# A fused transformer kernel: ties at the 32nd score found by counting, and one stage's weights loaded a stage earlier

## The chip, the cores and the metric

The kernel runs on one core of a Trainium2 chip, as one program of five instruction streams: TensorE (PE in the rows, PEld its weight loads), VectorE (DVE), ScalarE (ACT), GpSimd (POOL) and SyncE (SP, which only issues transfers). The metric is the device time of one execution in microseconds; lower is better. The kernel before took 2199.34 us in the median of three runs (2195.12 to 2203.02).

## The reference, cut to what matters

Six blocks follow each other, each on a layer norm of the running sum `x` (4 batches of 256 tokens, 256 wide):

```python
x = x + _L0_xattn_ref(_layernorm(x), ctx_768, ...)   # cross attention
x = x + _L0_attn_ref(_layernorm(x), ...)             # linear attention, a scan over tokens
x = x + _L0_ffn_ref(_layernorm(x), ...)              # 8 experts with low-rank parts
x = x + _L1_xattn_ref(_layernorm(x), ctx_768, ...)   # top-32 cross attention, S4D
x = x + _L1_attn_ref(_layernorm(x), ...)
x = x + _L1_ffn_ref(_layernorm(x), ...)
```

The change touches the fourth block's attention. There each query of each of 4 heads scores 4096 context rows, keeps the 32 best and takes their softmax:

```python
scores = jnp.einsum('bthd,bghd->bhtg', Q, K) / np.sqrt(DH)
topv, topi = jax.lax.top_k(scores, K_TOP)            # K_TOP = 32
probs = jax.nn.softmax(topv, axis=-1)
attn = jnp.zeros_like(scores).at[bi, hi, ti, topi].set(probs)
attn_mean = attn.mean(axis=1)                        # over the heads
c_t = jnp.einsum('btg,bgd->btd', attn_mean, V)
```

The expert block picks one expert for each token by the largest logit. The S4D part of the fourth block needs a convolution kernel that depends on weights alone; it is computed early, beside the experts.

## The kernel before, in words

`build` makes a list of stages: `stage_x0` (first cross attention), `stage_hla` (linear attention), `stage_moe` (experts, the S4D kernel, and the first keys of the next stage), `stage_x1a` (selection), then `stage_x1b` and `stage_a1`. Each stage has one function per engine. Between stages, `stage_end` lets every engine wait until all of them are done. Nothing is reordered: each engine runs its instructions as the code writes them, and waits on semaphores (`e.wait_ge`) are written by hand. SP issues its transfers in its own order, with waits of the same kind.

**Experts (`stage_moe`).** A list `plan`, made by `woven`, interleaves four strands: the experts of two batches, again two batches, the S4D kernel, and the keys ("keys" jobs, 8 chunks of 512 columns). SP begins with three loads of packed weights: `x1a` (weights of the keys), `moe` and `s4d`. Then it issues the context for the key chunks (`key_projection`, tiles `CT0` and `CT1` in turn, each waiting until the product that read it two pieces before is done). In the plan, DVE does the norms of two batches first, then the S4D set-up (`z_dt` on ACT, `z_pi` on DVE), then the first angle, then the gate's arithmetic (L1338). PE does two key chunks, transposes, two key chunks, then the gate products.

**Selection (`stage_x1a`).** There are 16 passes `p`: 4 batches x 2 halves of the tokens x 2 pairs of heads. A pass has two heads `h` with 128 queries in the partitions. PE computes 128x4096 scores per head and ACT copies them to SBUF (`SC`, two buffers). For each head DVE takes the 8 largest of each of 32 groups of 128 scores (`candidates`, L1674, results in `CA`, 128x256), and then `top` finds the 32 largest among the 256 candidates: MAX8 gives 8 values, MATCH_REPLACE overwrites these with `SENT`, and so on. `top` in the kernel before goes four rounds past the first MAX8, so that it has 40 values, and sets a flag where the 33rd value is not below the 32nd (a tie) or where some group of 128 holds 8 values that all reach the 32nd (a group may then hold more). PE adds up the flags of both heads over the partitions, DVE reads the sum into a register (`check`), and if it isn't zero a slow branch selects again with full-width passes. ACT computes the exponentials into `PM` (`weigh`), and DVE's `select` (L1716) masks and sums them: `(SC >= 32nd value) * PM`, 4096 wide, for both heads. POOL then takes, for each head, the reciprocal of the sum (L1787), scales (L1792 or L1795, into `ACC` or in place) and adds to `ACC` (L1797).

DVE's order for step `n`: candidates of pass `n-1`, first head; within them, after group 16 or 32, `check` and `select` of pass `n-2`; `top`; the second head's candidates; `top`. The select of an odd pass comes after 16 of the 32 groups, that of an even pass after all 32. Before three of the steps DVE converts a mask (L1667, 32x128), before three others it normalises a batch for the next queries (L1660).

## Time and profile before

| | us |
|---|---|
| median of 3 runs | 2199.34 |
| profiled execution | 2203.82 |
| its span, first to last instruction | 2202.0 |

| stretch, us from the span's start | what | length |
|---|---|---|
| to 889 | first cross attention | 889 |
| 889 to 1092.4 | linear attention (DMA share 0.01 between 1000 and 1060) | 203 |
| 1092.4 to 1250 | experts, S4D kernel, first keys | 158 |
| 1250 to about 1834 | selection | 584 |
| to 2202 | the rest | 368 |

Over the whole span PE is busy for 82%, DVE 56%, ACT 47%, POOL 35%. Such shares say little by themselves: each stretch has its own limit, and what a change is worth is read in its own stretch. A row of a timeline gives the start and the length of an instruction (or of several alike, with their count), and in brackets how long the engine was idle before it and what ended that. Idle time of an engine that isn't the bottleneck costs nothing.

### The profile page before, as it was taken

The page shows a single profiled execution, that of the slowest core. Times are in us where ns is not written, and L with a number is a line of the kernel's source. Part 1 is how long each engine was busy: PE and PEld are TensorE (multiplying, and loading weights), DVE is VectorE, ACT ScalarE, POOL GpSimd, SP SyncE. Part 2 cuts the span into 40 slices and gives each one's busy share as a digit, 9 for nine tenths or more (in the row PEclk, how much of TensorE's full clock was granted, in tenths as well). Part 3 has the DMA queues.
Part 4 walks back from the last instruction along what each step waited for, and adds up shares of the span by engine and source line. Part 5 has one row for each costly group of instructions (what it writes and reads, how often), then busy time and mean ns, then how long its engine had stood idle before and what let it go on. Part 6 is the DMA issues. An engine that isn't in the chain of part 4 may idle for free. (4 is left out here: it accounts for less than half of the span.)

```text
span 2202.0 us, 34851 instructions
## 1 busy us (share of the span) xinstructions
PE 1807.5 (82%) x13676; PEld 1104.1 (50%) x13676; DVE 1233.7 (56%) x3075; ACT 1025.5 (47%) x1381; POOL 759.8 (35%) x669
## 2 busy tenths in 40 slices
PE   5969999999999898888687877877766849888874
PEld 2434554454445444556466723544444437676653
DVE  5142424333332300364578379899999995557675
ACT  1457657756765687112131145555546521214442
POOL 6343324433542230000030027777878850110000
PEclk8989999999999999999967855878787669999897
DMA  6647555655756170000120001223132252000000
GB/s 143 118 105 127 117 109 109 117 119 113 122 109 128 56 125 38 1 2 1 58 70 1 14 1 44 79 59 87 51 86 66 58 184 86 1 1 1 1 6 15
DMA packets 78046, 150.01 MB, mean 68 GB/s; under 512 B 15464, under 2 KB 63144, under 8 KB 71464
## 3 DMA queue, kind: packets, MB, share of 16 engines
q1 hardware_dynamic: 64304, 101.80, 16.5%
q0 software_dynamic: 12768, 42.59, 12.7%
q8 instruction: 118, 1.93, 0.4%
q10 hardware_dynamic: 792, 3.17, 0.4%
q14 instruction: 64, 0.52, 0.1%
HBM read 93.59 MB, written 2.62 MB: 44 GB/s over the span
## 5 line engine op out<-in xcount | busy, mean ns | idle before, releaser
L571 ACT ACTIVATE P<-R 128x1024 f32<-128x1024 f32 x512 | 506.8, 1026 | 222.3 <-PE R L112 186.3
L112 PE MATMUL R<-QS,KST 100*128 100x256 bf16 x2048 | 297.0, 277 | 60.2 <-ACT P L571 53.5
L112 PEld LDWEIGHTS R<-QS,KST 100*128 100x128 bf16 x2048 | 170.0, 98 | 224.8 <-ACT P L571 120.9
L1797 POOL TENSOR_TENSOR ACC<-ACC,PM 128x4096 f32<-128x4096 f32 x22 | 195.2, 8872 | 1.8
L200 POOL TENSOR_TENSOR LNrs<-LNve,pk_const 128x2 f32<-128x2 f32 x36 | 25.3, 703 | 462.7 <-DVE LNve L196 462.5
L112 PE MATMUL R<-OV,QT 32*128 32x512 f32 x512 | 183.0, 802 | 0.0
L789 POOL DMA_DIRECT2D KST<-OV x300 | 144.5, 490 | 71.7 <-PE R L112 55.2
L112 PE MATMUL R<-P,VP 128*32 128x256 f32 x2304 | 156.1, 388 | 5.3 <-issue 5.0
L601 DVE CAST OV<-RT 128x512 bf16<-128x512 f32 x64 | 27.7, 432 | 217.2 <-ACT RT L116 130.0
L733 POOL CAST OV<-RT 128x512 bf16<-128x512 f32 x64 | 42.6, 665 | 266.5 <-DVE RT L604 266.5
L1787 POOL TENSOR_TENSOR SM<-SM,NG 128x1 f32<-128x1 f32 x30 | 79.3, 2644 | 147.5 <-DVE PM L1716 147.5
L112 PE MATMUL B<-P,VP 128*32 128x256 f32 x1792 | 121.2, 388 | 0.0
L1674 DVE MAX8 CA<-S 128x8 f32<-128x128 f32 x512 | 101.8, 275 | 12.0 <-ACT S L116 11.6
L1674 DVE MAX8 CA<-SC 128x8 f32<-128x128 f32 x512 | 100.9, 277 | 4.8 <-ACT SC L116 4.1
L116 ACT ACTIVATE S<-R 128x1024 f32<-128x1024 f32 x64 | 64.1, 1023 | 60.1 <-DVE PM L1716 34.3
L112 PEld LDWEIGHTS R<-P,VP 128*32 128x32 f32 x2304 | 60.7, 109 | 61.9 <-issue 36.2
L112 PE MATMUL R<-OV,ONB 1*128 1x512 bf16 x256 | 62.9, 488 | 33.9 <-ACT SC L116 20.8
L112 PEld LDWEIGHTS R<-OV,QT 32*128 32x128 f32 x512 | 65.1, 251 | 38.7 <-issue 30.9
L112 PE MATMUL R<-CN,AT 128*128 128x192 f32 x288 | 67.0, 385 | 19.1 <-DMA CN<-in_ctxn 13.6
L116 ACT ACTIVATE SC<-R 128x1024 f32<-128x1024 f32 x64 | 64.1, 1020 | 39.6 <-PE R L112 24.3
L1795 POOL TENSOR_SCALAR PM<-PM,SM 128x4096 f32<-128x4096 f32 x22 | 80.9, 3679 | 2.2
L1716 DVE SCALAR_TENSOR_TENSOR PM<-SC,T,PM 128x4096 f32<-128x4096 f32 x16 | 71.1, 4484 | 9.8 <-ACT S L116 4.2
(370 smaller groups left out, 3559.0 us busy)
## 6 DMA issues: line engine op xcount, KB each, us to landing
KST<-OV POOLq DMA_DIRECT2D x276, 128.0 KB, 10.8
CT<-in_ctxP SPq DMA_DIRECT2D x40, 768.0 KB, 4.4
CN<-in_ctxn SPq DMA_DIRECT2D x60, 384.0 KB, 3.5
CT<-in_ctxT SPq DMA_DIRECT2D x64, 192.0 KB, 2.5
KST<-OV SPq DMA_DIRECT2D x84, 128.0 KB, 10.4
KST<-in_ctxP ACTq DMA_DIRECT2D x4, 768.0 KB, 9.4
QS<-x_q POOLq DMA_DIRECT2D x24, 128.0 KB, 5.4
pk_a<-in_pk_a SPq DMA_DIRECT2D x1, 3014.0 KB, 10.4
```

Source lines behind the costliest of these rows:

```text
L112: return e.matmul(o, l, r, start=st, stop=sp, skip_group_check=True)
L116: return e.activation(o, i, ACT.Copy)
L200: return e.tensor_tensor(LNrs[:, i, :], LNve[:, i, :], cst["nhalf"], ALU.pow)
L571: e.activation(P[(32 * p + k0) % 3][:, :], ring.at(("s", p, k0))[:, :], ACT.Exp).then_inc(*EX.up((p, k0)))
L601: e.tensor_copy(KS[0][:, cs], rt[:, :]).then_inc(*KD.up())
L733: e.tensor_copy(KS[1][:, cs], rt[:, :]).then_inc(*KG.up())
L789: e.dma_start(KST[buf][16 * s:16 * s + 16, hh, cols], KS[SLOT_K[s]][r0:r0 + 16, cols]).then_inc(*S[buf].up((b, g) if hh == hs[-1] and s == ...
L1674: e.max(CA[:, g * 8:g * 8 + 8], SC[p % 2][:, h, g * 128:g * 128 + 128]).then_inc(*V.up())
L1716: e.scalar_tensor_tensor(pm[:, :], SC[p % 2][:, h, :], T8[p % 2][:, h, 31:32], pm[:, :], ALU.is_ge, ALU.mult, accum_out=SM[p % 3][:, h, SU ...
L1787: e.tensor_tensor(rc, sm[:, h, SUM:SUM + 1], NG1[:, :], ALU.pow).then_inc(*G.up())
L1795: e.tensor_scalar(pm, pm, rc, 0.25, ALU.mult, ALU.mult).then_inc(*G.up())
L1797: e.tensor_tensor(acc[:, :], acc[:, :], pm, ALU.add).then_inc(*G.up(("sum", p, h)))
```

## The change

In `top`, the fourth round (MATCH_REPLACE and MAX8) goes. In its place a TENSOR_SCALAR compares all 256 remaining candidates with the 32nd value and adds up the result along the row. 24 of the 32 largest have been overwritten by then, so the count is 8 where there is no tie. The last instruction becomes a SCALAR_TENSOR_TENSOR, which compares the largest eighth value of a group with the 32nd, as before, and adds the count. Summed over 128 rows and two heads, the value without ties or full groups is 2 x 128 x 8, and `check` compares with that.

In `stage_moe`, the three loads and the context of the first key chunk move to a new function, `moe_loads`, whose `sync` SP runs in `stage_hla`. Its order is `s4d`, `x1a`, `moe`, context. The tiles are allocated ahead of the linear attention's and kept through both stages. `key_projection` takes the PSUM slots as an argument of its functions; its instructions are the same.

```diff
-        def stage_hla(c):
+        def stage_hla(c, loads):
 ...
             def sync(e):
-                pass
+                loads(e)
 ...
+        def moe_loads(c, x1a):
+            t = {nm: pack(c, nm) for nm in ("moe", "s4d")}
+            keys = key_projection(c, x1a[1])
+            LW, W4 = dsig("w_moe"), dsig("w_s4d")
+
+            def sync(e):
+                load(e, "s4d", t["s4d"][0], W4)
+                load(e, "x1a", x1a[0], LA)
+                load(e, "moe", t["moe"][0], LW)
+                keys["sync"](e, 0, 0)
+
+            return dict(t, keys=keys, LW=LW, W4=W4, sync=sync)
 ...
             def sync(e):
-                load(e, "x1a", x1a[0], LA)
-                load(e, "moe", t_moe, LW)
-                load(e, "s4d", t_s4, W4)
                 for kind, *at in plan:
-                    if kind == "keys":
+                    if kind == "keys" and at[1] > 0:
                         keys["sync"](e, *at)
 ...
-                    for r8 in range(4):
+                    for r8 in range(3):
                         if r8 > 0:
                             e.wait_ge(*V.now())
                         e.match_replace(CA[:, :], t8[:, 8 * r8:8 * r8 + 8], CA[:, :], SENT).then_inc(*V.up())
                         e.wait_ge(*V.now())
                         e.max(t8[:, 8 * r8 + 8:8 * r8 + 16], CA[:, :]).then_inc(*V.up())
+
                     e.wait_ge(*V.now())
-                    e.tensor_scalar(fl, fl, t8[:, 32:33], t8[:, 31:32], ALU.max, ALU.is_ge).then_inc(*V.up(("fl", p, h)))
+                    e.tensor_scalar(CA[:, :], CA[:, :], t8[:, 31:32], 0.0, ALU.is_ge, ALU.add, accum_out=t8[:, 32:33]).then_inc(*V.up())
+                    e.wait_ge(*V.now())
+                    e.scalar_tensor_tensor(fl, fl, t8[:, 31:32], t8[:, 32:33], ALU.is_ge, ALU.add).then_inc(*V.up(("fl", p, h)))
 ...
-                    with e.If_ne(reg["v"], 0):
+                    with e.If_ne(reg["v"], 2 * 128 * 8):
```

On DVE, the end of `top` for the first pass and head stands like this before (`CA` are the candidates, `T_143` the values found, `SM_145` holds the flag):

```order
L1686 MATCH_REPLACE CA<-T_143,CA 128x256 [waits x1_select]
L1688 MAX T_143<-CA 128x8 [waits x1_select]
L1686 MATCH_REPLACE CA<-T_143,CA 128x256 [waits x1_select]
L1688 MAX T_143<-CA 128x8 [waits x1_select]
L1690 TENSOR_SCALAR SM_145<-SM_145,T_143 128x1 [waits x1_select]
L1674 MAX CA<-SC_127 128x8 [waits x1_copy,x1_select]
```

and like this in the changed kernel:

```order
L1696 MATCH_REPLACE CA<-T_143,CA 128x256 [waits x1_select]
L1698 MAX T_143<-CA 128x8 [waits x1_select]
L1701 TENSOR_SCALAR CA,T_143<-CA,T_143 128x256 [waits x1_select]
L1703 SCALAR_TENSOR_TENSOR SM_145<-SM_145,T_143 128x1 [waits x1_select]
L1684 MAX CA<-SC_127 128x8 [waits x1_copy,x1_select]
```

One MATCH_REPLACE and one MAX are replaced by the count, and the last instruction before the next candidates has two tensors as inputs, `SM_145` and a column of `T_143`, beside the scalar from `T_143`. Before, it had one tensor and two scalars.

On SP, at the end of the first cross attention, before (`OV<-in_pk_hla` is the linear attention's weights, issued in the first stage):

```order
L222 DMA OV<-in_pk_hla 128x4864 [waits d_k_slots1,d_k_slots_pool1,d_k_slots_pool0,d_k_slots0]
L222 DMA pk_x1a<-in_pk_x1a 128x512 [waits stage_end_tensor,stage_end_vector,stage_end_gpsimd,stage_end_scalar]
L222 DMA pk_moe<-in_pk_moe 128x5512
L222 DMA pk_s4d<-in_pk_s4d 128x1291
L1067 DMA CT_91<-in_ctxT 96x2x256
L1067 DMA CT_92<-in_ctxT 96x2x256
L1067 DMA CT_91<-in_ctxT 96x2x256 [waits x1_key_product]
```

and in the changed kernel:

```order
L222 DMA OV<-in_pk_hla 128x4864 [waits d_k_slots1,d_k_slots_pool1,d_k_slots_pool0,d_k_slots0]
L222 DMA pk_s4d<-in_pk_s4d 128x1291 [waits stage_end_scalar,stage_end_gpsimd,stage_end_vector,stage_end_tensor]
L222 DMA pk_x1a<-in_pk_x1a 128x512
L222 DMA pk_moe<-in_pk_moe 128x5512
L1082 DMA CT_52<-in_ctxT 96x2x256
L1082 DMA CT_53<-in_ctxT 96x2x256
L1082 DMA CT_52<-in_ctxT 96x2x256 [waits stage_end_gpsimd,stage_end_scalar,x1_key_product,stage_end_vector,stage_end_tensor]
```

The waits for the ends of the stages show where the boundary lies: the five transfers stand behind the first boundary only, and the sixth behind the second as well.

## Rows read from the trace of the kernel before

**Rows 1.** Windows view, 1250:1850: busy us (count) by engine, clock, DMA share.

```profile
1250.00:1850.00 600.00, 444.52 (x1879) 268.47 (x1880) 526.04 (x1695) 300.58 (x269) 389.03 (x89) 0.73 0.24 74
```

**Rows 2.** Timeline, DVE, one odd and one even pass: start us, length us.

```profile
1604.59 4.49 DVE L1716 SCALAR_TENSOR_TENSOR PM<-SC,T,PM 128x4096 f32<-128x4096 f32 x1 [0.59 <-DVE FI L1697]
...
1620.23 0.09 DVE L1686 MATCH_VALUE_LOAD CA<-T,CA 128x8 f32 x1
...
1621.21 0.27 DVE L1690 TENSOR_SCALAR SM<-SM,T 128x1 f32<-128x1 f32 x1
...
1621.52 6.29 DVE L1674 MAX8 CA<-S 128x8 f32<-128x128 f32 x32
...
1632.42 0.27 DVE L1690 TENSOR_SCALAR SM<-SM,T 128x1 f32<-128x1 f32 x1
...
1639.65 4.52 DVE L1716 SCALAR_TENSOR_TENSOR PM<-S,T,PM 128x4096 f32<-128x4096 f32 x1 [0.59 <-DVE FI L1697]
...
1653.19 0.27 DVE L1690 TENSOR_SCALAR SM<-SM,T 128x1 f32<-128x1 f32 x1
...
1664.40 0.27 DVE L1690 TENSOR_SCALAR SM<-SM,T 128x1 f32<-128x1 f32 x1
...
1669.38 4.49 DVE L1716 SCALAR_TENSOR_TENSOR PM<-SC,T,PM 128x4096 f32<-128x4096 f32 x1 [1.44 <-ACT S L116]
```

**Rows 3.** Timeline, POOL, the same stretch.

```profile
1617.75 8.91 POOL L1797 TENSOR_TENSOR ACC<-ACC,PM 128x4096 f32<-128x4096 f32 x1
...
1627.27 3.69 POOL L1795 TENSOR_SCALAR PM<-PM,SM 128x4096 f32<-128x4096 f32 x1
...
1631.04 8.84 POOL L1797 TENSOR_TENSOR ACC<-ACC,PM 128x4096 f32<-128x4096 f32 x1
...
1652.79 0.55 POOL L1787 TENSOR_TENSOR SM<-SM,NG 128x1 f32<-128x1 f32 x1
...
1657.20 8.89 POOL L1797 TENSOR_TENSOR ACC<-ACC,PM 128x4096 f32<-128x4096 f32 x1
```

**Rows 4.** Timeline, all engines, start of the expert stage.

```profile
1097.21 0.73 DVE L204 TENSOR_SCALAR XN<-X,LNmv,LNrs 128x256 f32<-128x256 f32 x2 [0.81 <-POOL LNrs L200]
...
1104.23 0.42 ACT L1212 ACTIVATE z_dt<-pk_s4d 128x256 f32<-128x256 f32 x1 [16.57 <-DMA pk_s4d<-in_pk_s4d]
...
1104.75 0.42 DVE L1292 TENSOR_TENSOR z_pi<-z_dt,pk_s4d 128x256 f32<-128x256 f32 x1 [6.81 <-ACT z_dt L1212]
...
1109.61 0.43 DVE L1246 TENSOR_TENSOR z_den<-z_t,z_t 128x256 f32<-128x256 f32 x1
...
1120.34 0.57 ACT L116 ACTIVATE OV<-B 128x512 f32<-128x512 f32 x1
...
1122.26 3.47 PE L112 MATMUL B<-pk_moe,XT 128*128 128x40 f32 x16
...
1124.13 0.24 DVE L1338 TENSOR_TENSOR LG<-B,pk_moe 128x80 f32<-128x80 f32 x1 [4.88 <-PE B L112]
```

**Rows 5.** Groups by line and form, DVE: busy us, mean ns.

```profile
L1716 DVE DVE_READ_ACCUMULATOR PM<-S,T,PM 128x1 f32 x16 | 1.3, 81 | 0.0
...
L1300 DVE TENSOR_SCALAR z_nden<-z_den 128x256 f32<-128x256 f32 x1 | 0.3, 293 | 0.0
```

**Rows 6.** One source line, L647: ns min/median/max.

```profile
L647 DVE TENSOR_TENSOR BW<-KMX,QMX x8: 149/159/987, 42.3 to 770.3; 128x1 f32<-128x1 f32 x8
```

**Rows 7.** Timeline, POOL and DVE, 42:44.

```profile
42.16 1.15 POOL L735 TENSOR_TENSOR OV<-RT,OV 128x512 bf16<-128x512 f32 x1
42.34 0.99 DVE L647 TENSOR_TENSOR BW<-KMX,QMX 128x1 f32<-128x1 f32 x1
```

**Rows 8.** Timeline, POOL and DVE, near 1599.

```profile
1591.88 8.88 POOL L1797 TENSOR_TENSOR ACC<-ACC,PM 128x4096 f32<-128x4096 f32 x1
...
1599.27 1.57 DVE L1667 TENSOR_SCALAR MR<-MU 32x128 bf16<-32x128 uint8 x1
```

**Rows 9.** DMA issues: KB, median us to landing.

```profile
pk_moe<-in_pk_moe SPq DMA_DIRECT2D x1, 2756.0 KB, 9.2
```

More of the change, by code:

```diff
@@ L1051, in sync, with key_projection @@
             def sync(e):
-                pass
+                loads(e)
             return dict(tensor=tensor, vector=vector, scalar=scalar, gpsimd=gpsimd, sync=sync, slots=(ring, bank))
-        def key_projection(c, w, bank):
+        def moe_loads(c, x1a):
[8 more added lines that the diff above has]
+            return dict(t, keys=keys, LW=LW, W4=W4, sync=sync)
+        def key_projection(c, w):
             K1 = OV[:, 0:NK]
@@ L1067, in sync, with tensor @@
                     e.dma_start(CT[n % 2][:, :, :], src).then_inc(*CT1[n % 2].up(n))
-            def tensor(e, b, ch):
+            def tensor(e, bank, b, ch):
                 ps, free = bank.take(("k", b, ch), (KC1, (b, ch)))
@@ L1077, in tensor, with scalar @@
                     mm(e, o, w["Wk"][0:96, 1, :], CT[n % 2][:, 1, :], False, True).then_inc(*KM1.up(n))
-            def scalar(e, b, ch):
+            def scalar(e, bank, b, ch):
                 e.wait_ge(*KM1.at(16 * b + 2 * ch + 1))
@@ L1083, in key_projection, with stage_moe @@
             return dict(tensor=tensor, scalar=scalar, sync=sync)
-        def stage_moe(c, x1a):
-            t_moe, w = pack(c, "moe")
+        def stage_moe(c, early):
+            w, ws, keys, LW, W4 = early["moe"][1], early["s4d"][1], early["keys"], early["LW"], early["W4"]
             XN = [sbt(c, f"XN{i}", [128, 2, 256]) for i in range(2)]
@@ L1094, in stage_moe @@
             ring, bank = Slots(R), Slots(B2)
-            keys = key_projection(c, x1a[1], bank)
-            t_s4, ws = pack(c, "s4d")
             zs = ["dt", "pr", "pi", "den", "nden", "nr", "t0", "t1", "cr", "ci", "dr", "di", "b0"]
@@ L1105, in stage_moe @@
             z = {k: v[:, :] for k, v in Z.items()}
-            M, V, S, NP, GZ, LW = sig("moe_product"), sig("moe_vector"), sig("moe_inter"), sig("moe_root"), sig("moe_zero"), dsig("w_moe")
-            W4, V4, S4, G4, M4 = dsig("w_s4d"), sig("s4d_vector"), sig("s4d_function"), sig("s4d_outer"), sig("s4d_kernel")
+            M, V, S, NP, GZ = sig("moe_product"), sig("moe_vector"), sig("moe_inter"), sig("moe_root"), sig("moe_zero")
+            V4, S4, G4, M4 = sig("s4d_vector"), sig("s4d_function"), sig("s4d_outer"), sig("s4d_kernel")
             s4_steps = 15
@@ L1142, in tensor @@
                             e.wait_ge(*LA.at("x1a"))
-                        keys["tensor"](e, *at)
+                        keys["tensor"](e, bank, *at)
                     elif kind == "s4d" and at[0] == "kernel":
@@ L1208, in scalar @@
                     if kind == "keys":
-                        keys["scalar"](e, *at)
+                        keys["scalar"](e, bank, *at)
                     elif kind == "s4d" and at[0] == "setup":
@@ L1419, in stage_x1a @@
             ring, bank = Slots(R[0:2]), Slots([B2[0], B2[1], R[2][:, 0:512], R[2][:, 512:1024]])
-            keys = key_projection(c, w, bank)
+            keys = key_projection(c, w)
             K1, MRT = OV[:, 0:NK], OV[:, NK:NK + NK // 2].bitcast(BF16)
@@ L1576, in tensor @@
                         if n % 4 == 0 and rekeyed(n, ch):
-                            keys["tensor"](e, *rekeyed(n, ch))
+                            keys["tensor"](e, bank, *rekeyed(n, ch))
                         if n < NP:
@@ L1580, in tensor @@
                         if n % 4 == 3 and rekeyed(n, ch):
-                            keys["tensor"](e, *rekeyed(n, ch))
+                            keys["tensor"](e, bank, *rekeyed(n, ch))
                         if m is not None and n % 2 == 0 and ch in (1, 3, 5, 7):
@@ L1642, in scalar @@
                         if n % 4 == 0 and rekeyed(n, ch):
-                            keys["scalar"](e, *rekeyed(n, ch))
+                            keys["scalar"](e, bank, *rekeyed(n, ch))
                         if n < NP:
@@ L1646, in scalar @@
                         if n % 4 == 3 and rekeyed(n, ch):
-                            keys["scalar"](e, *rekeyed(n, ch))
+                            keys["scalar"](e, bank, *rekeyed(n, ch))
                         if m is not None and n % 2 == 0 and ch in (3, 5):
@@ L2592, in build @@
             stages.append(stage_x0(c))
-        with ExitStack() as c:
-            stages.append(stage_hla(c))
         KL = sbt(ctx, "KL", [128, 2, 256])
         x1a = pack(ctx, "x1a")
-        with ExitStack() as c:
-            stages.append(stage_moe(c, x1a))
+        with ExitStack() as both:
+            early = moe_loads(both, x1a)
+            with ExitStack() as c:
+                stages.append(stage_hla(c, early["sync"]))
+            with ExitStack() as c:
+                stages.append(stage_moe(c, early))
         CS = sbt(ctx, "CS", [128, 2 * NB, 192])
```

## The prediction

> **What bounds the kernel now.** I read the time of each stretch first, then the timeline of VectorE (DVE) in the two stretches that the change touches, then GpSimd (POOL) beside it. The selection stage lies between 1250 and 1850 us. DVE is busy 526 of its 600 us, PE 445, POOL 389, ACT 301 [rows 1], so DVE sets the pace, and the reader is to see that POOL is busy two thirds of the time beside it. DVE's order repeats every two passes [rows 2]. In an odd pass the masked sums ("select", L1716) come in the middle of the first candidate sweep, in an even pass at its end. From the select at 1604.59 (odd) to the one at 1639.65 (even) it is 35.06 us, from there to 1669.38 it is 29.73. DVE hardly idles; before 1669.38 it waits 1.44 for ACT.
>
> Each select releases POOL, which then runs without a gap [rows 3]: a small power instruction, a scaling (3.7 us), a 4096-wide addition (8.9), and for the second head all three again. After the odd select it ends at 1639.88, where the even select has just begun. So POOL's chain (35.3 from select to end) is as long as DVE's half period (35.06).
>
> The expert stage starts at 1092.4 with nothing loaded. ACT's first instruction waits for the S4D pack until 1104.23, DVE starts its S4D arithmetic at 1104.75 although its norms were done at 1097.94 [rows 4].
>
> **The change, part by part.**
>
> *Fourth round removed.* A round is MATCH_VALUE_LOAD, MATCH_REPLACE and MAX8: from 1620.23 to 1621.21, 0.98 us. The flag instruction L1690 goes too, 0.31 by the start of the next one [rows 2]. Removed: 1.29 us in each of 32 calls of `top`, 41.3 us of DVE.
>
> *Count added.* A TENSOR_SCALAR of 128x256 with an accumulated output. No row shows this form. Below it lies the plain one at 0.29 [rows 5], above it an instruction with two inputs of this width, 0.43 [rows 4]. I take 0.42 (the upper row, since the one accumulated form that the trace has, the select, runs at one element a cycle: 4.49 us for 4096), plus 0.08 for reading the accumulator [rows 5], plus 0.1 to the next start: 0.6.
>
> *Combining flag added.* A SCALAR_TENSOR_TENSOR of 128x1 on the flag and the count, both in SBUF. By itself 0.16, the median of L647's 128x1 TENSOR_TENSOR [rows 6], 0.25 with the gap. If nothing interfered, `top` would be 1.29 - 0.6 - 0.25 = 0.44 us shorter, 14 us in all.
>
> It is interfered with. L647 runs eight times: 0.16 in the median, 0.99 at most [rows 6]. The longest starts at 42.34 while POOL adds from 42.16 to 43.31, and ends at 43.33, with POOL's instruction [rows 7]. So a DVE instruction with two SBUF tensor inputs, however small, waits for the whole POOL instruction in flight. The selection shows the same for another form: the 32x128 mask conversion L1667 takes 1.57 beside an addition on POOL from 1591.88 to 1600.76 and ends with it [rows 8]. The old flag instruction had one tensor and pointer scalars and took 0.27 in the middle of POOL's additions (at 1621.21, 1632.42 and 1664.40 [rows 2, 3]): it was not held. The new one, with two tensors, stands exactly there. Behind it in DVE's queue are all candidates, the next select, and by that POOL, ACT's copies into the score buffer and PE's flag product.
>
> The odd half: three rounds end at 1620.23, the count takes 0.6, and the flag wants to start at 1620.85. POOL adds from 1617.75 to 1626.66 [rows 3]: a wait of 5.8. The next candidates start at 1626.9, not 1621.52 (+5.4). The second `top` arrives 5.4 later, less 0.4 saved, so its flag wants to start at 1637.4; POOL's second addition ends at 1639.88, moved 0.2 by the flag let in before it: a wait of 2.7. Candidates start at 1640.3, not 1632.73. The half is longer by 7.6. There are seven (passes 1, 3, ... 13; pass 15 has no successor on POOL): 7 x 7.6 = 53.
>
> The even half: the first flag wants to start at 1652.8, at a small power instruction (1652.79, 0.55 [rows 3]): at most 0.5 lost, as much as was saved. The second wants 1664.0 and POOL adds until 1666.09: a wait of 2.2, candidates 1.7 later. But before the next select DVE waited 1.44 for ACT, which hides that, and in five of the eight even halves a conversion or a norm already waits for this same addition [rows 8], so that they grow by only 0.3. I take 4 for all. Selection: +57, with 49 to 62 as its bounds: 7 x 6.7 to 7 x 8 (the count from 0.29 to 1.0 shifts little, since it lies under the wait; POOL's next instruction may slip in first, 0.6), and 2 to 6 for the even halves. PE and ACT, busy 445 and 301 of 600, get more slack, not less.
>
> The Trainium skill, "SBUF — State Buffer", Who interferes with whom, says that a TENSOR_SCALAR which also writes out its accumulator stays out of the two-port mode, and so would not be held by POOL; no run here shows it. By the rule the count costs what I put down; were it to behave like L1667, the rival below holds.
>
> *Loads moved.* In the expert stage SP issues three packs and the first keys' context. They now go at the start of the linear attention, which lasts 203 us, with a DMA share of 0.01 in the middle of it (the table above). SP has nothing else queued there, and waits at the stage's end in any case. I cost the four pieces at nothing: the largest has 2756 KB and lands in 9.2 us [rows 9]. If that cover were gone, at worst all of these 9.2 us would fall on the linear attention's start and take the gain below with them. At the expert stage's start, DVE goes on to S4D at 1097.95 in place of 1104.75: 6.8 gained. The 4.88 us that it waited before L1338 are for the gate product; this waits for ACT's copy of keys (1120.34), which sits behind ACT's sines, which wait for DVE. All these move by 6.8, but PE is then early: the gate product can start at the copy's end (1120.9 - 6.8 = 1114.1) rather than at 1122.26 [rows 4], so it gains 8.2. I take 8; bounds 0 (the cover gone) and 11.7 (6.8 and all of the 4.88). After that PE, ACT and DVE hand on to each other and all move alike.
>
> **Sum.** Against the profiled execution, 2203.8 (span 2202.0 and 1.8 around it): + 57 - 8 = 2252.8. It is 4.5 above the median of the three runs, 2199.3, so the median comes out at 2199.3 + 49 = 2248.
>
> **Rivals.**
> 1. *Small flags aren't held* (L647's 0.99 would then be chance). For: a single instance. Against: it ends with POOL's instruction to 0.02 us, and the 0.84 too much are too large for noise. Then DVE has 14 us less. But POOL's chain of 35.3 leaves the odd halves where they are, since the select has two SBUF tensors itself and would wait for it; and the masks and norms wait for the end of the addition anyway. That leaves some 1 us for each of the three last even halves: -2.5 - 8 = -10.5, 2189. This is the faster side, and it decides by one thing: the wait of the 128x1 form. If nothing were held, not even the select, it would be -14 - 8, 2177.
> 2. *The count is held too*, by using both ports like L1667. It then waits first, POOL's next instruction slips in, and the flag waits again. What changes is that the count's own 0.5 us no longer lies under the wait, in some 28 of the 32 calls: 14 more, 2262.
> 3. *The fall-back runs*, because the count isn't 2048 in sum over both heads. The branch has 16 full-width instructions for each pass; at the select's 4.4 us each, 70 us a pass, and above 3300 for all 16. The diff's arithmetic gives 8 per row and head without ties, so I give it 2 in 100.
> 4. *The waits cancel*: the added 7.6 lie where PE and ACT were already late, or the early loads disturb less than they save. Price: around 2205. For it speaks only that DVE idles a few us per pass; against it that it hardly idles in the rows.
>
> **Chances.** Forecast 0.74, rival 1 0.13, rival 2 0.08, rival 3 0.02, rival 4 0.03. The forecast's own range is 2236 to 2258. With 2 in 10 left out the range takes in rival 2 and the lower end of the main case: 2226 to 2266. A change of 0.3% (6.6 us) is what the measurement can tell. Slower: forecast, rivals 2 and 3, 0.84; same: 0.03; faster: 0.13.
>
> **What would show it.** Right: 32 flag instructions of 128x1 whose durations are mostly 2 to 6 us and end with POOL's additions; odd halves of 42 to 43 us; L1667 no longer near 1.6; 96 MATCH_REPLACE; counts at 0.4 to 0.5. Expert stage: S4D's first DVE instruction 5.5 us after the stage's start (was 12.4), the stage 8 us shorter, the linear attention unchanged. Wrong: flag instructions of 0.2 us beside a busy POOL, or DVE idle for ACT or PE where I have it held.

## The result and the profile after

| | before | after |
|---|---|---|
| median of the paired runs, us | 2198.47 (4 runs) | 2235.97 (2234.02 to 2238.47, 4 runs) |
| ratio | | 1.017, 95% interval 1.0147 to 1.0192 |
| profiled execution / its span | 2203.82 / 2202.0 | 2234.31 / 2232.5 |
| linear attention | 203.1 | 201.6 |
| expert stage | 158.6 | 149.8 |
| selection | 582.9 | 630.8 |
| the rest | 368.0 | 365.4 |

The change costs 37.5 us, 1.7%. I had forecast +49. Both terms show: the selection is 47.9 longer (forecast 57), the expert stage 8.9 shorter (forecast 8; from DVE's last addition to `X` in one stage to that in the next it is 157.92 before and 149.07 after). The two profiled executions differ by 30.5, less than the medians: the one after was quicker by 8.6 ahead of and behind the two stages, 4.5 of it in the first cross attention, whose code is the same.

The selection by engine, as in [rows 1], now from 1250 to 1850 of the changed kernel:

```profile
1250.00:1850.00 600.00, 417.26 (x1713) 247.67 (x1710) 561.62 (x1592) 291.29 (x254) 384.10 (x82) 0.70 0.22 66
```

DVE is busy 562 of 600 in place of 526, with fewer instructions (1592 for 1695), and PE, ACT and POOL do less in the same time. "Busy" includes the time in which an instruction has started and is held; a higher share is not more work.

DVE's instructions of the selection in the changed kernel, grouped (busy us, mean ns of one):

```profile
L1703 DVE SCALAR_TENSOR_TENSOR SM<-SM,T 128x1 f32<-128x1 f32 x32 | 84.1, 2630 | 1.1
...
L1696 DVE MATCH_REPLACE8 CA<-T,CA 128x256 f32<-128x256 f32 x96 | 39.2, 409 | 0.0
L1701 DVE TENSOR_SCALAR_CACHE_REDUCE CA<-CA,T 128x256 f32<-128x256 f32 x32 | 15.3, 479 | 1.1
```

One element per partition, 32 times, is 84.1 us, more than twice what all 96 MATCH_REPLACE of 256 elements cost. The count has a mean of 479 ns.

One odd half of the changed kernel on DVE, which answers to [rows 2]:

```profile
1320.36 4.48 DVE L1729 SCALAR_TENSOR_TENSOR PM<-SC,T,PM 128x4096 f32<-128x4096 f32 x1 [0.91 <-DVE FI L1710]
...
1335.99 0.48 DVE L1701 TENSOR_SCALAR_CACHE_REDUCE CA<-CA,T 128x256 f32<-128x256 f32 x1
1336.52 5.87 DVE L1703 SCALAR_TENSOR_TENSOR SM<-SM,T 128x1 f32<-128x1 f32 x1
1342.42 6.29 DVE L1684 MAX8 CA<-S 128x8 f32<-128x128 f32 x32
...
1352.86 2.76 DVE L1703 SCALAR_TENSOR_TENSOR SM<-SM,T 128x1 f32<-128x1 f32 x1
1355.65 6.28 DVE L1684 MAX8 CA<-SC 128x8 f32<-128x128 f32 x32
...
1362.88 4.48 DVE L1729 SCALAR_TENSOR_TENSOR PM<-S,T,PM 128x4096 f32<-128x4096 f32 x1 [0.90 <-DVE FI L1710]
```

and POOL beside it, which answers to [rows 3]:

```profile
1324.94 4.72 POOL L1800 TENSOR_TENSOR SM<-SM,NG 128x1 f32<-128x1 f32 x1 [8.79 <-DVE PM L1729]
...
1333.52 8.85 POOL L1810 TENSOR_TENSOR ACC<-ACC,PM 128x4096 f32<-128x4096 f32 x1
...
1346.74 8.86 POOL L1810 TENSOR_TENSOR ACC<-ACC,PM 128x4096 f32<-128x4096 f32 x1
```

Add start and length. The first flag ends at 1342.39, POOL's first addition at 1342.37; the second flag ends at 1355.62, the second addition at 1355.60. From the flag's start to the addition's end it is 5.85 and 2.74 (forecast 5.8 and 2.7). So it is with all: of the 32 flags 22 take 2.6 to 5.9 us, and each of these ends 0.01 to 0.03 us after an addition of POOL; the other ten take 0.22 and meet no addition. POOL is idle 8.79 before it starts: it waits for the DVE that it holds up later. The count at 1335.99 runs in the middle of the same addition and isn't held.

The holding goes both ways. POOL's first small instruction, 128x1 with two inputs in SBUF, takes 4.72 at 1324.94, beside DVE's second select, where its neighbours of the same shape take 0.55. The "35.3 from select to end" of POOL's chain includes these 4 us too.

The start of the expert stage, after, which answers to [rows 4] (the last instruction of the linear attention on DVE is the first row):

```profile
1085.52 0.69 DVE L1043 TENSOR_TENSOR X<-B,X 128x512 f32<-128x512 f32 x1 [5.89 <-PE B L112]
...
1091.84 0.42 DVE L1305 TENSOR_TENSOR z_pi<-z_dt,pk_s4d 128x256 f32<-128x256 f32 x1
...
1108.26 0.24 DVE L1351 TENSOR_TENSOR LG<-B,pk_moe 128x80 f32<-128x80 f32 x1 [3.75 <-PE B L112]
```

`z_pi` follows the norms with no wait. The gate's arithmetic (L1351) starts 22.7 after that first row, where it was 32.6 before (1091.54 to 1124.13 in [rows 4]).

### The profile page after: what moved, and what is told of

Read it like the earlier page. It is cut to its first block, busy times and chain, and to the rows that moved or that the text cites. A ratio compares the mean times of both kernels' runs of the same rounds, so it can differ in the third digit from the quotient of the medians.

```text
span 2232.5 us, 34819 instructions
## 1 busy us (share of the span) xinstructions
PE 1811.9 (81%) x13676; PEld 1108.1 (50%) x13676; DVE 1286.1 (58%) x3043; ACT 1025.9 (46%) x1381; POOL 760.7 (34%) x669
## 4 chain that ended last, share of the span: by engine, by line
PE 47%; DVE 31%; ACT 10%; issue 5%; POOL 3%; DMA 3%; DVEq 0%; ACTq 0%; POOLq 0%
PE R L112 30%; PE B L112 15%; DVE CA L1684 7%; ACT P L571 7%; DVE PM L1729 6%; DVE SM L1703 3%; POOL KST L789 2%; DMA KST<-OV 2%; DVE CA L1696 2%; DVE T L1698 2%; PE B L178 1%; ACT PS L2367 1%; DVE RT L604 1%; ACT RT L116 1%; DMA CN<-in_ctxn 1%
## 5 line engine op out<-in xcount | busy, mean ns | idle before, releaser
L112 PE MATMUL R<-OV,QT 32*128 32x512 f32 x512 | 188.2, 823 | 0.0
L1703 DVE SCALAR_TENSOR_TENSOR SM<-SM,T 128x1 f32<-128x1 f32 x32 | 84.1, 2630 | 1.1
L116 ACT ACTIVATE SC<-R 128x1024 f32<-128x1024 f32 x64 | 64.0, 1020 | 38.7 <-PE R L112 22.7
```

The costliest lines, as they stand in the source:

```text
L112: return e.matmul(o, l, r, start=st, stop=sp, skip_group_check=True)
L116: return e.activation(o, i, ACT.Copy)
L1703: e.scalar_tensor_tensor(fl, fl, t8[:, 31:32], t8[:, 32:33], ALU.is_ge, ALU.add).then_inc(*V.up(("fl", p, h)))
```

## The experiments

Twelve kernels, with the kernel before run beside each. The two columns on the right are parts of the profiled execution: the selection, here from DVE's last addition to `X` in the expert stage to the first scaling of `OV` after the selection (1.7 more than in the table above, by its start), and the last stretch, from there to the end of the span.

| kernel | time, us | ratio to before | selection | last stretch |
|---|---|---|---|---|
| before | | 1 | 584.6 | 368.0 |
| after | 2235.97 | 1.017 (1.0147 to 1.0192) | 632.5 | 365.4 |
| e1 scalar flag | 2183.96 | 0.9942 (0.9928 to 0.9956) | 581.2 | 365.1 |
| e2 loads only | 2188.57 | 0.9954 (0.9940 to 0.9969) | 585.1 | 367.9 |
| e3 old rounds, two-tensor flag, late loads | 2247.78 | 1.0224 (1.0210 to 1.0238) | 632.9 | 367.6 |
| e4 POOL's addition in quarters | 2186.05 | 0.9951 (0.9937 to 0.9965) | 585.3 | 364.7 |
| e5 scalar flag and quarters | 2182.37 | 0.9932 (0.9906 to 0.9957) | 581.4 | 365.3 |
| e6 scalar flag, late loads | 2190.03 | 0.9967 (0.9956 to 0.9979) | 581.5 | 365.1 |
| e7 POOL's addition in halves | 2207.09 | 1.0037 (1.0022 to 1.0051) | 605.5 | 365.1 |
| e8 old rounds, early loads, quarters | 2195.66 | 0.9998 (0.9986 to 1.0011) | 590.1 | 368.2 |
| e9 scalar flag, half of the addition | 2178.42 | 0.9906 (0.9878 to 0.9935) | 577.9 | 365.4 |
| e10 old rounds, early loads, half of the addition | 2184.05 | 0.9934 (0.9912 to 0.9956) | 579.8 | 368.3 |
| e11 scalar flag, 32 fillers | 2182.44 | 0.9938 (0.9921 to 0.9954) | 582.5 | 364.3 |
| e12 scalar flag, 8 fillers | 2180.66 (one run) | | 581.3 | 365.2 |

The kernels ran in four groups (e1 to e4, e5 to e8, e9 and e10, e11 and e12), so ratios are compared across groups, not times.

### Is it the form of the flag?

**e1**, the changed kernel with one line changed:

```diff
-e.scalar_tensor_tensor(fl, fl, t8[:, 31:32], t8[:, 32:33], ALU.is_ge, ALU.add)
+e.tensor_scalar(fl, fl, t8[:, 31:32], t8[:, 32:33], ALU.is_ge, ALU.add)
```

> The changed kernel with one instruction in another form: the flag is combined by a TENSOR_SCALAR with the 32nd value and the count as pointer scalars, instead of a SCALAR_TENSOR_TENSOR with two SBUF tensors. Same values, same waits. Theory (a DVE instruction with two SBUF tensors waits for the whole POOL instruction in flight): the 32 flags take 0.27 us each, the selection falls from 630.8 us to 580 (the 583 of before, less some 3 for the round saved, since POOL's chain sets the odd halves), the kernel comes to 2198 - 9 - 3 = 2186 (2182 to 2191). Rival (the count itself, 0.56 us with its accumulator, and the extra semaphore hop are what costs): the time stays near 2236.

Measured 2183.96. The groups of e1 in the selection:

```profile
L1701 DVE TENSOR_SCALAR_CACHE_REDUCE CA<-CA,T 128x256 f32<-128x256 f32 x32 | 15.3, 479 | 1.1
L1703 DVE TENSOR_SCALAR SM<-SM,T 128x1 f32<-128x1 f32 x32 | 8.7, 273 | 1.2
```

The same two values reach the instruction, the count now through a pointer scalar in place of a tensor operand. The flags fall from 84.1 to 8.7 us and the kernel by 52. The count stays at 479: it was never held.

**e3**, the kernel before with only the form of its flag changed:

```diff
-e.tensor_scalar(fl, fl, t8[:, 32:33], t8[:, 31:32], ALU.max, ALU.is_ge)
+e.scalar_tensor_tensor(fl, fl, t8[:, 32:33], t8[:, 31:32], ALU.max, ALU.is_ge)
```

> The kernel before with one instruction in another form: its flag (four rounds, no count, late loads) is a SCALAR_TENSOR_TENSOR with two SBUF tensors instead of a TENSOR_SCALAR with two pointer scalars. Same values. Theory: as the saved 0.4 us per call lie under the waits, this form alone costs 50 (45 to 57): 2248, flags of 5.5, 2.5, 0.3 and 2.5 us in turn. Rival (the count is needed for the loss): 2198 and flags of 0.3 us.

Measured 2247.78, against 2198.09 before in the same group: +49.7. The group of e3:

```profile
L1690 DVE SCALAR_TENSOR_TENSOR SM<-SM,T 128x1 f32<-128x1 f32 x32 | 70.2, 2193 | 1.1
```

The form alone makes the loss, on a kernel with no other change. Together e1 and e3 settle it from both sides. They change the operation and the number of tensor operands at once; that it is the operands is argued, from the TENSOR_TENSOR of 128x1 in [rows 7], which was held as well.

**e2**, the changed kernel with the old selection, so the early loads alone:

> The changed kernel with the selection of the kernel before (four rounds, old flag); only the loads are early. Theory: expert stage 149.8 us as in the changed kernel (158.7 before), all else as before: 2198 - 9 = 2189 (2186 to 2193). Rival (the linear attention pays for the transfers, or later stages give the gain back): 2198.

Measured 2188.57, 9.5 under the kernel before in its group (by the interval of the ratio 7 to 13).

**e6**, the other half: the selection of e1, with the loads issued at the start of the expert stage, in the old order:

> The count with the scalar flag, and the loads issued at the start of the expert stage in the order of the kernel before. Theory: the two parts of the change add up, so that the time is that of the scalar flag with early loads (2184) plus the 8.9 that the expert stage lost: 2192.5 (2190 to 2196), expert stage at 158 to 159, S4D's first DVE instruction 12.4 after its start, selection at 579.6. Rival, that part of the gain seen in the expert stage is given back or taken elsewhere (transfers on top of the linear attention, other addresses in SBUF): the time is below 2188 or above 2197, with the difference outside of the expert stage.

Measured 2190.03, at the edge of the range. By the ratios it is 5.5 above e1 (by their intervals 1.5 to 9.5) where I expected 8.9. The expert stage took 156.0 in e6's profile (from DVE's last addition to `X` in the linear attention to its last one in the expert stage), 147.7 in e1's and 157.9 in before's, so that e6 and e1 differ by 8.3 there. Its first S4D instruction starts 12.8 after the stretch's start (13.2 before). But the gate's arithmetic in e6 came 30.2 after the start and not 32.6. PE, the gate products in before and in e6:

```profile
1122.26 3.47 PE L112 MATMUL B<-pk_moe,XT 128*128 128x40 f32 x16
```

```profile
1114.37 1.98 PE L112 MATMUL B<-pk_moe,XT 128*128 128x40 f32 x16 [0.36 <-ACT OV L116]
```

The same products take 3.47 at a granted clock of 0.50 and 1.98 at 1.00. In e6 the clock was at 1.00 in the two groups of key products ahead of them too; in before it was 0.79 in the first of these and 0.56 in the second. So the early loads are worth 5.5 to 9.5, by which neighbour they are taken against, and e6's expert stage is 1.9 shorter than that of before, which comes with the higher clock.

### Does a held instruction wait for the POOL instruction in flight?

**e7 and e4** cut POOL's addition of 4096 columns into two of 2048 and four of 1024, and keep the two-tensor flag:

```diff
-e.tensor_tensor(acc[:, :], acc[:, :], pm, ALU.add).then_inc(*G.up(("sum", p, h)))
+for q4 in range(4):
+    qs = slice(q4 * NK // 4, (q4 + 1) * NK // 4)
+    e.tensor_tensor(acc[:, qs], acc[:, qs], pm[:, qs], ALU.add).then_inc(*G.up(("sum", p, h) if q4 == 3 else None))
```

> The changed kernel with its two-tensor flag, POOL's 4096-wide addition as two of 2048 (4.5 us each). Theory: a held flag ends with the POOL instruction in flight, so no flag takes over 4.6 us, and they end with the first or the second half of an addition; total of the flags between the 26.6 us of quarters and the 84.1 of whole additions, 40 to 60; time between 2186 and 2236, 2200 (2192 to 2212). Rival, that a held instruction waits until POOL has nothing more to do, or for a fixed time: durations as in the changed kernel, or the same in halves and quarters (up to 1.7).

> The changed kernel with POOL's 4096-wide addition as four of 1024, one after another with no wait between them; the two-tensor flag stays. Theory (the hold lasts as long as the one POOL instruction in flight): no flag takes over 2.5 us, and the kernel is at 2200 (2193 to 2210), POOL's chain being some 0.5 us longer per addition. Rival (the hold lasts until POOL's queue is empty, or it is something else): flags up to 5.9 us, 2236 or more.

Measured 2207.09 in halves, 2186.05 in quarters. The flags' groups of e7 and of e4:

```profile
L1703 DVE SCALAR_TENSOR_TENSOR SM<-SM,T 128x1 f32<-128x1 f32 x32 | 56.0, 1751 | 1.1
```

```profile
L1703 DVE SCALAR_TENSOR_TENSOR SM<-SM,T 128x1 f32<-128x1 f32 x32 | 26.6, 830 | 1.1
```

The flags take 84.1, 56.0, 26.6 us for whole, half and quarter instructions, and 2236, 2207, 2186 for the kernel. In e7 a flag and POOL's two halves (9.02 us for both) look like this:

```profile
1611.36 1.55 DVE L1703 SCALAR_TENSOR_TENSOR SM<-SM,T 128x1 f32<-128x1 f32 x1
```

```profile
1608.37 9.02 POOL L1812 TENSOR_TENSOR ACC<-ACC,PM 128x2048 f32<-128x2048 f32 x2
```

The flag ends at 1612.91, and the first half, half of 9.02 from 1608.37, at 1612.88. DVE gets in between two POOL instructions; a held instruction waits for one instruction, not for the end of POOL's work. The longest flags fall from 5.9 to 2.9 and 1.7. POOL pays little for the cut: 9.3 for four quarters in place of 8.87.

e4 beat my 2200 because the even halves fell too, those without keys from 30.3 to 28.4: their second flag's wait of 2.7 is also cut, to 0.8, and I had counted the odd halves alone.

### Why is the saved round worth so little once the flag is cured?

The count takes 0.42 us per `top` off DVE, 13.4 in all (DVE's busy time in e9 against e10, below). Against e2 (old rounds) e1 is only 4.6 faster, 2.6 by the ratios. Three pairs that differ by the count alone:

| POOL's addition | with the count | old rounds | difference of ratios x 2198 | difference of the selections |
|---|---|---|---|---|
| whole | e1, 0.9942 | e2, 0.9954 | 2.6 (4.4 either way) | 3.8 |
| in quarters | e5, 0.9932 | e8, 0.9998 | 14.5 (6 either way) | 8.8 |
| half left out | e9, 0.9906 | e10, 0.9934 | 6.2 (8 either way) | 1.9 |

Only the middle difference of ratios is clear of the noise. The selections of the profiles tell more, and each pair differs by another 2.9 in the last stretch (the last experiments below).

> The changed kernel with both cures: the flag as a TENSOR_SCALAR with two pointer scalars, and POOL's 4096-wide addition as four of 1024. With the scalar flag alone the odd halves were 34.13 from the start of one select to the next, but the even select was then held 0.94 us by POOL's addition, so that from end to end it is 35.07: POOL's chain still bounded them. With the quarters alone they were 36.16, of which 2.0 are waits of the flags. Theory: with both, nothing on DVE waits more than a quarter of an addition, so odd halves are 34.1 to 34.3, even halves 28 (28.4 less 0.6 of flags' waits), and the kernel is 16 to 20 us below the 2186 of the quarters alone, less 3 to 8 us of waits for ACT and PE that come back: 2172 (2166 to 2180). Rival, that POOL's chain bounds the halves whether cut up or not (its additions in quarters take 9.3 in place of 8.9, 36.1 for the chain): odd halves stay at 36.1 and the time at 2184 to 2186, in spite of flags of 0.27.

> The old selection (four rounds, old flag) with the early loads, and POOL's addition in quarters. It completes a square with the loads only (2189), the scalar flag (2184) and both cures together. Theory: the count saves 0.4 us per call where POOL no longer holds DVE, 14 us in all, of which 2184 against 2189 shows only 5, because the select is held by POOL's addition there. So here the time is 8 to 14 us above that of the scalar flag with quarters: 2183 (2178 to 2188). Rival, that the small gain of the count lies in waits for ACT and PE, which the quarters don't change: the difference between the two kernels with quarters is again 5 us or less.

e5 took 2182.37, not 2172, and e8 2195.66, not 2183. Both theories of e5 are off in part. The first: the odd halves are 34.14 from start to start, as expected, but the select that follows is held. A select of e1 and one of e5, each the first of an even pass:

```profile
1621.32 5.45 DVE L1729 SCALAR_TENSOR_TENSOR PM<-S,T,PM 128x4096 f32<-128x4096 f32 x1 [0.59 <-DVE FI L1710]
```

```profile
1619.06 6.28 DVE L1729 SCALAR_TENSOR_TENSOR PM<-S,T,PM 128x4096 f32<-128x4096 f32 x1 [0.59 <-DVE FI L1710]
```

An undisturbed one takes 4.48. In e1 34.13 and 0.97 of holding make 35.10, the 35.06 of the kernel before: DVE is earlier, and meets POOL's last addition. In e5 34.14 and 1.80 make 35.94, since POOL in quarters needs 0.9 longer, and DVE comes at the last quarter. So POOL's chain from select to select bounds the odd half, in one piece or in four. That was the step in the prediction's first rival. In e8 the old rounds come at 35.06, into the same last quarter, and lose up to 0.8 there. In the kernel before they come just when POOL is through (4.52 in [rows 2]). By this luck e2's selection is 5 us shorter than e8's (the holds of e8's selects sum to 5.1), and so the pair in quarters shows more than the others; the whole difference between e2 and e8 is 9.7 by the ratios, 4.2 either way, and what lies beyond the 5 isn't explained.

The selects are not all that is held. The mask conversions and the norms of the queries in the selection (TENSOR_SCALAR, 32x128 and 128x256) have one tensor as input, and still end with POOL's additions. The three conversions beside an addition take 1.5 to 1.6 each in e2 and 2.4 to 2.5 in e1, where 0.21 is undisturbed; the two norms beside one take 1.6 to 1.7 in e2 and 2.6 in e1, where 0.41 is undisturbed. From e2 to e1 the holds grow by 5.8 for the selects, 2.8 for the conversions and 1.9 for the norms: 10.4 of the 13.4 that the count takes off. DVE's busy time in the selection falls by 3.2 alone (515.4 to 512.2). So with whole additions most of the saving goes into waits for POOL.

**e9 and e10** take the load away. POOL adds only the first 2048 columns to `ACC`:

```diff
-e.tensor_tensor(acc[:, :], acc[:, :], pm, ALU.add).then_inc(*G.up(("sum", p, h)))
+e.tensor_tensor(acc[:, 0:NK // 2], acc[:, 0:NK // 2], pm[:, 0:NK // 2], ALU.add).then_inc(*G.up(("sum", p, h)))
```

> The changed kernel with the scalar flag, and POOL adds only the first 2048 of 4096 columns to ACC (the sum over the heads is left out for the others): its chain from a select to the end of the second addition falls from 35.3 to about 26.5 us. Theory: POOL's chain bounds the selection with the scalar flag from two sides, the even select (held up to 1.8) and PE's transposes of ACC (PE waits 6.7 to 8.7 for POOL's last addition every second pass, and its score products behind them feed ACT and so DVE). With the short chain both go: odd halves 34.1 with selects of 4.5, even halves about 28, 62 for two passes in place of 65.3, 7.5 times, so 2160 (2154 to 2168), and PE no longer waits for POOL. Rival, that PE's or ACT's own work bounds the two passes at 65: no more than 4 us faster than the 2184 of the whole addition.

> The old rounds and the old flag with the early loads, and the same half addition on POOL (the sum over the heads left out for the other columns). Theory: where POOL's chain doesn't bound, the count is worth what it takes off DVE, 0.4 us in each of 32 calls: this kernel is 11 to 15 us slower than the one with the count and the same addition, so 2173 if that one is at 2160. Rival, that the count's saving is hidden in the selection by something else than POOL's chain: they differ by 5 us or less, as with the whole addition (2189 against 2184).

2178.42 and 2184.05: my theory, 2160 and 11 to 15 between them, fell, and so did the picture of POOL as the only bound. The selects are at 4.48, the conversions at 0.20 and the norms at 0.41, and PE no longer waits for POOL (46.7 us in e1), as expected. But DVE now waits for others. DVE's waits in the selection, e9 (who waits, for whom: us in all, times, longest):

```profile
DVE CA L1684 <- ACT S L116: 11.6, 8, 2.9
...
DVE PM L1729 <- ACT PM L1614: 7.0, 4, 2.4
DVE CA L1684 <- ACT SC L116: 6.0, 3, 3.6
DVE FI L1710 <- PE B L112: 5.9, 2, 5.5
...
DVE FI L1710 <- PE R L112: 5.4, 2, 3.0
DVE PM L1729 <- ACT S L116: 4.1, 2, 2.7
```

and e10:

```profile
DVE CA L1684 <- ACT S L116: 11.2, 8, 2.4
...
DVE FI L1707 <- PE B L112: 4.3, 2, 3.9
DVE CA L1684 <- ACT SC L116: 4.1, 2, 3.6
DVE PM L1726 <- ACT S L116: 3.7, 2, 2.2
DVE PM L1726 <- ACT PM L1614: 2.4, 1, 2.4
```

They sum to 40.0 and 25.7. DVE is busy 13.4 less in e9 (495.4 against 508.8) and waits 14.3 more for ACT and PE; with its other idle time counted it idles 11.5 more, and the selection is 1.9 shorter. The even halves with keys wait most: 35.9, 33.7 and 32.2 in e9, where those without keys take 25.2 to 28.8. Two windows of e9, without and with keys (us, then PE, PEld, DVE, ACT and POOL busy, the granted clock, DMA share, GB/s):

```profile
1285.00:1313.00 28.00, 16.32 (x46) 5.12 (x42) 24.15 (x71) 13.38 (x11) 17.13 (x5) 0.50 0.00 1
1349.00:1385.00 36.00, 32.88 (x132) 21.57 (x131) 29.16 (x95) 18.16 (x20) 17.13 (x5) 0.75 0.36 101
```

PE is busy 32.9 of 36 in the second. So the saved DVE time is to be had only where neither POOL's chain nor PE and ACT bound the half; that PE, and not ACT, bounds those with keys is argued from this busy share. In the averages of [rows 1], PE is at 74% and looks free.

### A gain of 2.7 us in a stage that wasn't changed

In the table's last column the kernels with the count have 364.3 to 365.4, all nine, and those with the old rounds 367.6 to 368.3, all five. The last stage (`stage_a1`) holds the difference. DVE, the same two instructions in before, then in e1:

```profile
2161.38 0.17 DVE L2426 TENSOR_SCALAR q_SCL<-q_AM 128x16 f32<-128x16 f32 x1
2162.01 0.23 DVE L2426 TENSOR_SCALAR q_SCL<-q_SCL,EDA 128x16 f32<-128x16 f32 x1 [0.46 <-DVE q_SCL L2426]
```

```profile
2140.52 0.17 DVE L2439 TENSOR_SCALAR q_SCL<-q_AM 128x16 f32<-128x16 f32 x1
2140.81 0.23 DVE L2439 TENSOR_SCALAR q_SCL<-q_SCL,EDA 128x16 f32<-128x16 f32 x1
```

and PE behind them, before and e1:

```profile
2164.38 3.08 PE L178 MATMUL B<-pk_const,PS 128*128 128x128 f32 x12 [2.09 <-DVE PS L2529]
2168.24 1.51 PE L112 MATMUL B<-PT,VN 128*32 128x256 f32 x16 [0.78 <-ACT PT L116]
2170.33 5.50 PE L112 MATMUL B<-pk_a,YT 128*128 128x256 f32 x16 [0.58 <-ACT YT L116]
```

```profile
2143.18 3.08 PE L178 MATMUL B<-pk_const,PS 128*128 128x128 f32 x12 [1.74 <-DVE PS L2542]
2147.03 0.86 PE L112 MATMUL B<-PT,VN 128*32 128x256 f32 x16 [0.78 <-ACT PT L116]
2148.48 3.69 PE L112 MATMUL B<-pk_a,YT 128*128 128x256 f32 x16 [0.58 <-ACT YT L116]
```

Before, DVE stops for 0.46 where it waits for nothing that the profile names. PE then idles 2.09 in place of 1.74. The transposes behind this gap take 3.08 in both kernels, for the granted clock is down beside them in both: 0.50 from 2164 to 2168 before, 0.59 from 2143 to 2147 in e1. In e1 it is back at 1.00 from 2147 on, before the next products; in the kernel before it stays at 0.50 until 2174, and they take 1.51 for 0.86, and 5.50 for 3.69. 0.35 us of delay become 2.8. Since the count makes DVE's program 32 busy instructions shorter (3043 for 3075 in the execution), I put 32 small MEMSETs back (e11), and 8 as a control (e12), behind DVE's 18 us wait at the end of the selection (the 32 take 0.94):

```diff
+for i in range(32):
+    e.memset(DUM[:, i:i + 1], 0.0)
 e.wait_ge(*LB.at("x1b"))
```

> The scalar flag kernel with 32 small MEMSETs (128x1, of a tile of their own) on DVE at the end of the selection, where DVE waits 18 us for a transfer, so that DVE has as many instructions ahead of the last stage as before. Every kernel with the old rounds shows one stop of 0.46 us in DVE's stream at L2436 q_SCL in the last stage, without anything that it waits for, then PE starts a group of transposes 0.35 later, and two groups of products behind it run at half the granted clock (1.51 and 5.50 us in place of 0.86 and 3.69): 2.7 us in all, in five kernels of five; none of the seven with the count shows it. Theory: the stop belongs to the place of the instruction in DVE's stream. Then it comes back here: 0.46 idle before q_SCL, the stretch from the end of the selection to the end 367.7 to 368.3 in place of 365.0 to 365.4, and the time 2186.5 (2184 to 2190). Rival, that it comes from what the old rounds do in the selection (their data or the times): the stretch stays at 365.

> The same with 8 MEMSETs, as the control for the new tile and the place of the fillers. Theory: the stop moves by 8 instructions or not at all, but doesn't fall on q_SCL as before; unless it happens to delay PE, the last stretch stays at 365.0 to 365.4. Rival, that the tile or the fillers in themselves bring it back: 367.7 to 368.3.

e11 took 2182.44, and its last stretch 364.3: the forecast of 2186.5 fell. The stop did come back, but smaller and one instruction later. DVE and PE of e11:

```profile
2143.34 0.25 DVE L2485 RECIPROCAL q_RCP<-q_SCL 128x16 f32<-128x16 f32 x1 [0.15 <-DVE q_SCL L2442]
```

```profile
2145.45 3.08 PE L178 MATMUL B<-pk_const,PS 128*128 128x128 f32 x12 [1.86 <-DVE PS L2545]
2149.30 0.86 PE L112 MATMUL B<-PT,VN 128*32 128x256 f32 x16 [0.78 <-ACT PT L116]
```

With 8 fillers there is none, and PE idles 1.75. So in these kernels the clock is back in time for the next products after a gap of 1.74 to 1.86 (in e11 it is 0.57 from 2145 to 2149 and 1.00 behind), and not after one of 2.09. The gap's length alone doesn't decide: one of 2.37 a little earlier, at 2161.43 before and at 2140.58 in e1, is followed by products at 0.86 in both. That the stop depends on where the instruction lies in DVE's program fits e11 and e12, but it isn't shown; what the stop is stays open.

## Why the prediction was right, and where its sizes were off

- *The main mechanism was right.* The 128x1 instruction with two SBUF tensors is held by the POOL instruction in flight (e1, e3, e4, e7). Rival 1 is out: no flag beside an addition takes less than the rest of it. Its time, 2189, was that of the cure: e1 has 2184. Rival 2 is out: all 32 counts take 478 to 481 ns. Rival 3 is out, since no fall-back instruction stands in the trace. Rival 4 was too large in price but has a true core, below. The total was missed by 11.5 of 49, and the terms that were off follow.
- *Odd halves: forecast +7.6 each, measured +7.1.* From select to select they sum to 296.5 in place of 246.6, +49.9 for seven. The waits were right to 0.1. The step that was off is the end of the second wait: I had the next candidates start 35.7 after the select (POOL's end, moved by 0.2 by the flag let in before it, and 0.2 for the flag itself behind it). The flag didn't move POOL and ended with it, and in the rows above it is 35.3 (1320.36 to 1355.65).
- *Even halves: forecast +4, measured -1.8 (eight sum to 241.7 in place of 243.5).* This is the term of the sum that was mis-sized, and it carries 5.8 of the 9 us missed in the selection. Six of the eight grew, by 4.1 in all, though the second flag waited 2.7 in place of 2.2. I had put nothing for the other two, which lost 5.9: where PE computes keys, DVE had waited for PE and ACT. Before, the select of pass 3 ([rows 2] show the mildest of these, the 1.44 before 1669.38):

```profile
1403.17 0.15 DVE L1697 CAST FI<-B 1x1 int32<-1x1 f32 x1 [2.44 <-PE B L112]
1405.72 4.49 DVE L1716 SCALAR_TENSOR_TENSOR PM<-SC,T,PM 128x4096 f32<-128x4096 f32 x1 [2.40 <-ACT PM L1604]
```

  After, the same select:

```profile
1393.64 4.49 DVE L1729 SCALAR_TENSOR_TENSOR PM<-SC,T,PM 128x4096 f32<-128x4096 f32 x1 [0.60 <-DVE FI L1710]
```

  That half falls from 34.9 to 30.8. The seven odd halves, 50 us slower, let PE and ACT get ahead, and 4.1 us come back here, 1.8 in the half of this kind four passes later. In e3, whose only change is the flag, the same two halves take 30.8 and 31.1 (before 34.9 and 32.9). So a part of rival 4 came true (the added time lies where PE and ACT were already late), worth 6 us and not the 43 between the forecast and the 2205 of that rival. I had written that PE and ACT "get more slack, not less", and put no number on it.
- *The count: forecast 0.6 from its start to the flag's, measured 0.53 (0.48 for the instruction; the reading of the accumulator lies half under it).* Right in size, and of no weight, since it lies under the wait. The Trainium skill ("SBUF — State Buffer", Who interferes with whom) says that the form of `tensor_scalar` which also writes out its accumulator stays out of the 2-port modes that contend with GpSimd. The trace agrees: 22 of the 32 counts ran beside an addition of POOL, and all took 478 to 481 ns.
- *The flag: 0.22 undisturbed, forecast 0.16.* The row that I took it from is of a TENSOR_TENSOR; without weight too.
- *Loads: forecast -8, measured -8.9 in the stage, and -9.5 for the kernel (e2).* The linear attention is unchanged (201.6 for 203.1), so the transfers were covered. The first S4D instruction comes 6.9 earlier (forecast 6.8). The step that was off is "ACT's sines wait for DVE". Before, they waited for ACT's own queue, in which the copies of `XT` stood behind PE's transposes, and these behind the key context; counted from DVE's last instruction of the stage before, the sines start 8.9 earlier, and the gate product 10.0. ACT's sines, before and after:

```profile
1118.20 1.06 ACT L1221 ACTIVATE zp_si<-zp_r 128x1024 f32<-128x1024 f32 x1
```

```profile
1103.28 1.06 ACT L1234 ACTIVATE zp_si<-zp_r 128x1024 f32<-128x1024 f32 x1 [5.57 <-DVE zp_r L1271]
```

- *Not in the forecast:* the 2.7 us in the last stage.
- *The sum.* Measured 48 - 9 - 3 = 36 by stages, and 37.5 by the medians, against 57 - 8 = 49. 2235.97 lies on the lower edge of the likeliest case's own range (2236 to 2258) and inside the full range.
- *The stated tests.* The flags came as described (5.87 and 2.76; even halves 0.22 and 2.63 to 2.74); odd halves 42.2 to 42.5; the mask conversion at 0.2 (no longer 1.57, as in [rows 8]); 96 MATCH_REPLACE; counts at 0.48; S4D's first instruction 5.4 after the stage's start.

Of the kernels that compute all of the result, e5 (0.9932) and e1 (0.9942; 0.9938 as e11, with the fillers) are the fastest, and beat both the kernel before and the changed one; their intervals overlap. e1 needs one line of the change written otherwise.

## What to carry to other kernels

Before a small instruction is put among large ones, count its operands in SBUF: on VectorE beside a busy GpSimd, one tensor and pointer scalars cost 0.27 us, and two tensors up to 5.9 us for the same element. One tensor alone is no warrant at other sizes: the mask conversion, 32x128, and the norm, 128x256, took 2.5 and 2.6 us beside GpSimd in e1, and 0.21 and 0.41 without it. Where such an instruction can't be avoided, cut GpSimd's long instruction into pieces, since the hold ends with the piece in flight. And when a wait grows on the engine that bounds, subtract what it was itself waiting for in the same loop, pass by pass and not from one typical pass; when work is taken off it, the gain ends at the next engine, which a stage's average doesn't show.

## What was not expected of the hardware

- The hold is to the instruction in both directions: GpSimd's 128x1 power takes 0.55 alone and 4.72 beside a select of 4.48 us.
- Cutting a 4096-wide GpSimd addition in four costs 0.4 to 0.5 us in 8.87, and takes 57.6 us off the flags' total (84.15 to 26.55).
- TensorE's granted clock fell to 0.50 at the same place in both kernels, and stayed down over the next products where the gap before it was 2.09 us in place of 1.74: 1.51 in place of 0.86 and 5.50 in place of 3.69. After one of 1.86 it did not. A delay of a third of a microsecond on another engine cost 2.8.
- One and the same saving on VectorE, 13.4 us of work, shortened the selection by 3.8, 8.8 and 1.9 us, by whether GpSimd's additions were whole, in quarters or half left out. With whole ones, 10.4 of it went into longer holds of other instructions, single-tensor TENSOR_SCALARs among them.
- VectorE stopped for 0.46 us between two instructions of one chain with nothing that it waited for, in all five kernels with the old rounds; with 32 fillers the stop is 0.15 and one instruction later. Its cause is open.
